# Expert products of a sparse feed-forward layer: Gelu reads them four at a time from the exponential's PSUM buffers

## The chip, the cores and the metric

The kernel runs on one core of a Trainium2 chip. The metric is the device time of the whole program in microseconds (us), lower is better. A core has the engines PE (TensorE, matmul), DVE (VectorE), ACT (ScalarE), POOL (GpSimd) and SP (SyncE, which issues the transfers here). Each runs its own instructions in order; semaphores tie them together.

## The reference

The input has 16 sequences of 512 tokens with 128 channels. An attention layer in a window comes first and is untouched by the change. The second layer, which is the subject, picks for each token and each of 8 heads the 8 best of 1024 experts by a product of keys, and sums the experts' outputs by softmax weights:

```python
sim = jnp.einsum('pbnhd,hkpd->pbnhk', q, keys)        # 2 x 8 heads x 32 keys for a token
s, i = jax.lax.top_k(sim, k)
all_scores = (sx[..., :, None] + sy[..., None, :])    # of the 8 best of either half
scores, pk = jax.lax.top_k(all_scores, k)
w_down, w_up = key_in[idx], key_out[idx]
o = jnp.einsum('bnd,bnhkd->bnhk', inputs, w_down)
o = jax.nn.gelu(o, approximate=False) * jax.nn.softmax(scores, axis=-1)
return jnp.einsum('bnhk,bnhkd->bnd', o, w_up)
```

## The kernel before

The attention stage takes some 700 us of the span; then `ffn` works through 64 tiles of 128 tokens, in 16 groups (`GROUPS`) of 4 tiles (`GT`). Nothing is gathered: all 1024 experts are computed for each token, and those not chosen get the weight zero. A tile j is tile k of group g (j = 4g + k); k = 0 and 2 are called even here, k = 1 and 3 odd.

For each tile and each of 8 heads h:

- POOL adds the 32 x 32 scores of the two halves into SUM (L795), in a ring of 16 buffers, so up to two tiles ahead. In odd tiles DVE makes the sum of the one head without a mask (L995).
- ACT takes the exponential, SUM to E (L922). E is two buffers in PSUM, used in turn, so the exponential n waits until DVE has read the one of n - 2.
- DVE compares SUM with the head's eighth best score and multiplies by E: W (L1029), called the masked product here.
- PE turns W's eight blocks of 128 x 128, summed over the heads, into WT (L1100), for all experts of the tile.

One head, `LH`, goes another way, without DVE: two passes of ACT over SUM, a shift (Prelu with a huge slope, L878, called at h = LH - 1) and the exponential (L884, at h = LH), which writes W itself. This is "the head without a mask".

At h = 1 of the next tile DVE multiplies WT by the Gelu of the expert products, GE, into CT (L1009). PE then multiplies CT by the experts' outputs (`outputs`, L1061 and L1064) into the PSUM bank MB, and ACT copies this to OUT (`finish`, L848). PE makes the next scores (`similar`, L1039) in MB too, and ACT copies them to SIM (L828). MB is a single bank: outputs, scores and expert products take turns in it, each waiting for the copy of the one ahead.

The expert products are key_in by X2T, 8 blocks (`BLK`) of 128 experts by the 512 tokens of a group, made one group ahead: two per tile (`o_block`, L1042, at h = 0 and h = 6) in MB. ACT copies each to GE (`o_copy`, L839, at h = 3 and, of the other, at h = 1 of the next tile). In the even tiles, behind the head without a mask, ACT loads the Gelu table, takes the Gelu of four copied products in one instruction of 2048 columns in place, and loads the exponential's table again (`gelus`, L834, L835). At h = 2 of tile k = 1 ACT makes BNT (L843), the next group's rows for `similar`.

The ranking of later tiles is done on DVE in ten parts (`choose`): copies of the eight best, candidates, maxima, sums, biases. The tables `EVEN_PARTS` and `ODD_PARTS` say ahead of which head's masked product each part stands. `SLOT_*` and `COPY_*` say ahead of which head PE makes a product in MB and ACT copies it. For the first group the products go to E before the loop starts, and Gelu reads them there (L856, L1052).

Of the kernel before, what the change touches and what calls it, by code (L numbers as in the profile page):

```python
# [29 lines left out]
ACT = mybir.ActivationFunctionType  # L30
# [3 lines left out]
P = 128  # L34
# [621 lines left out]
GT = 4  # L656
GN = GT * P
# [3 lines left out]
BLK = NE // P  # L661
# [1 line left out]
CAND = 20  # L663
RING = 16
WRING = 8
LH = 3
MASKED = FH - 1
SUMS_AHEAD = (0, 2)

EVEN_PARTS = ((), (), (), (), ((1, 0), (1, 1), (1, 2), (1, 3), (1, 4), (1, 5), (1, 8), (2, 0), (2, 1), (1, 9)), (), ((1, 6),), ((1, 7),))  # L670
ODD_PARTS = ((), (), ((1, 2),), ((1, 3),), ((1, 4), (1, 5)), (), ((1, 6),), ((1, 7),))

SIM0 = 2
SLOT_A, SLOT_OUT, SLOT_SIM, SLOT_B = 0, 2, 4, 6
COPY_B, COPY_A, COPY_OUT, COPY_SIM = 1, 3, 5, 7


def ffn(nc, ctx, x1, x2T, KM, key_in, key_out, gb, ident, bnst, first, out):
# [6 lines left out]
    def sem(name):  # L685
# [30 lines left out]
    E = [ps(f"E{b}", [P, NE]) for b in range(2)]  # L716
    WT = ps("WT", [P, BLK, P])
    MB = ps("MB2", [P, GN])
# [4 lines left out]

    names = ("waits_passed half_set bn_mean bn_variance bn_rstd bn_coef x1_loaded x2T_loaded bn_rows "
             "sim_product sim_copied pair_sums exp_ready weights_masked weights_turned "
             "experts_weighted out_product out_copied expert_product expert_copied gelu_ready "
             "out_stored ranked candidates top_ready top_less_max top_exp exp_sum log_sum bias_ready "
             "l_x_moved l_sums l_shifted l_weights").split()
    S = {n: sem("f_" + n) for n in names}
# [6 lines left out]
    def wait_pos(eng, s, v):  # L736

        if not isinstance(v, int) or v > 0:
            eng.wait_ge(s, v)
# [84 lines left out]
    def _(act):  # L824
# [2 lines left out]
            act.wait_ge(S["sim_product"], j + 1)  # L827
            nc.scalar.copy(SIM[q][:, :, :, :].rearrange("p a h k -> p (a h k)"), MB[:, :]).then_inc(S["sim_copied"], 1)  # L828

        def gelus(g, b, half):  # L830

            act.wait_ge(S["expert_copied"], g * BLK + (half + 1) * 4)
            o = GE[b][:, 4 * half:4 * half + 4, :].rearrange("p e n -> p (e n)")
            nc.scalar.activation(o, o, ACT.Gelu).then_inc(S["gelu_ready"], 1)  # L834
            nc.scalar.preload_act_table_set("natural_log_exp_and_others")  # L835

        def o_copy(g, b, e):
            act.wait_ge(S["expert_product"], g * BLK + e + 1)
            nc.scalar.copy(GE[b][:, e, :], MB[:, :]).then_inc(S["expert_copied"], 1)  # L839

        def bnt(g, b):
            act.wait_ge(S["x2T_loaded"], (g + 1) * 16)
# [9 lines left out]
        for e in range(BLK):  # L852
# [1 line left out]
                sim_copy(0, 0)  # L854
            act.wait_ge(S["expert_product"], e + 1)
            nc.scalar.activation(GE[0][:, e, :], E[e // 2 % 2][:, e % 2 * GN:(e % 2 + 1) * GN], ACT.Gelu).then_inc(S["expert_copied"], 1)  # L856
        act.wait_ge(S["expert_copied"], BLK)
        act.sem_inc(S["gelu_ready"], 2)
        nc.scalar.preload_act_table_set("natural_log_exp_and_others")
        sim_copy(1, 1)  # L860
        sim_copy(2, 2)
# [27 lines left out]
        def group(g, b, more):  # L889
            for k in range(GT):  # L890
                j = g * GT + k
                q = k % 2
                real = not (isinstance(g, int) and g == 0)
                nxt = more or k < GT - 1
                for h in range(FH):
                    if h == 0:
                        act.wait_ge(S["bias_ready"], j + 1)

                    if h == 2 and k == 1 and more:
                        bnt(g + 1, 1 - b)  # L900

                    if h == COPY_B and k and more:
                        o_copy(g + 1, 1 - b, 2 * k - 1)
                    if h == COPY_B and not k and real:
                        o_copy(g, b, BLK - 1)
                    if h == COPY_A and more:
                        if k == 0:
                            wait_pos(act, S["experts_weighted"], g * GT)
                        o_copy(g + 1, 1 - b, 2 * k)
                    if h == COPY_OUT and (real or k):  # L910
                        finish(j - 1, *((g, b, k - 1) if k else (g - 1, 1 - b, GT - 1)))
                    if h == COPY_SIM and (more or k < 1):
                        sim_copy(j + 3, (k + 3) % 4)
                    if h == LH - 1:
                        l_shift(j, k, q)
                    if h == LH:
                        l_exp(j, k, q)
                    else:
                        n = masked(j, h)
                        act.wait_ge(S["pair_sums"], sums_by_pool(j, h))  # L920
                        wait_pos(act, S["weights_masked"], n - 2)
                        nc.scalar.activation(E[(n - 1) % 2][:, :], SUM[(k * FH + h) % RING][:, :], ACT.Exp, bias=NB[q][:, h:h + 1]).then_inc(S["exp_ready"], 1)  # L922

                    if h == 5 and nxt:
                        small_exp(j + 1)
                    if h == 6 and nxt:
                        small_ln(j + 1)
                    if (k, h) == (2, 3) and more:
                        gelus(g + 1, 1 - b, 0)
                    if (k, h) == (0, 3) and real:  # L930
                        gelus(g, b, 1)

        steps(act, group)
        finish(GROUPS * GT - 1, GROUPS - 1, 1, GT - 1)
# [2 lines left out]
    def _(dve):  # L937
# [66 lines left out]
        def experts(j, g, b, k):  # L1004

            dve.wait_ge(S["weights_turned"], (j + 1) * FH)
            dve.wait_ge(S["gelu_ready"], (g + 1) * 2)
            wait_pos(dve, S["out_product"], j - 1)
            nc.vector.tensor_tensor(CT[k % 2][:, :, :], WT[:, :, :], GE[b][:, :, k * P:(k + 1) * P], ALU.mult).then_inc(S["experts_weighted"], 1)  # L1009

# [25 lines left out]
    def _(pe):  # L1036
# [1 line left out]

            pe.matmul(MB[:, :], BNT[b][:, k * P:(k + 1) * P], KM[:, :], start=True, stop=True).then_inc(S["sim_product"], 1)  # L1039

        def o_block(b, e):
            pe.matmul(MB[:, :], key_in[:, e * P:(e + 1) * P], X2T[b][:, :], start=True, stop=True).then_inc(S["expert_product"], 1)  # L1042


        for e in range(BLK):
# [21 lines left out]
        def group(g, b, more):  # L1067
            for k in range(GT):
                j = g * GT + k
                real = not (isinstance(j, int) and j == 0)  # L1070
                for h in range(FH):

                    if h == SLOT_A and more:
                        pe.wait_ge(S["x2T_loaded"], (g + 2) * 16)
                        pe.wait_ge(S["sim_copied"], j + 3)
                        pe.wait_ge(S["expert_copied"], (g + 1) * BLK + 2 * k)
                        o_block(1 - b, 2 * k)
                    if h == SLOT_OUT and real:
                        pe.wait_ge(S["sim_copied"], j + 3 if more or k < 2 else GROUPS * GT)
                        pe.wait_ge(S["expert_copied"], (g + 1) * BLK + (2 * k + 1 if more else 0))  # L1080
                        wait_pos(pe, S["out_copied"], j - 1)
                        outputs(j - 1, *((g, b, k - 1) if k else (g - 1, 1 - b, GT - 1)))
                    if h == SLOT_SIM and (more or k < 1):
                        pe.wait_ge(S["bn_rows"], (g + 1) if k < 1 else (g + 2))
                        pe.wait_ge(S["expert_copied"], (g + 1) * BLK + (2 * k + 1 if more else 0))
                        wait_pos(pe, S["out_copied"], j)
                        similar(j + 3, b if k < 1 else 1 - b, (k + 3) % GT)
                    if h == SLOT_B and more:
                        pe.wait_ge(S["sim_copied"], j + 4)
                        o_block(1 - b, 2 * k + 1)  # L1090
                    if h == LH:
                        pe.wait_ge(S["l_weights"], j + 1)
                    else:
                        pe.wait_ge(S["weights_masked"], masked(j, h))

                    if h == 0:
                        wait_pos(pe, S["experts_weighted"], j)

                    for e in range(BLK):
                        o = pe.matmul(WT[:, e, :], W[h % WRING][:, e * P:(e + 1) * P], ident[:, :], is_transpose=True,  # L1100
                                      start=(h == 0 and e % 4 == 0), stop=(h == FH - 1), skip_group_check=True)
                    o.then_inc(S["weights_turned"], 1)
# [62 lines left out]
```

## Time and profile before

| | us |
|---|---|
| median of 3 runs | 1681.59 (1681.23 to 1687.32) |
| profiled execution | 1680.84 |
| its span, first to last instruction | 1679.1 |

| Engine | busy us | share of span |
|---|---|---|
| DVE | 1476.9 | 88% |
| PE | 1467.7 | 87% |
| ACT | 1315.0 | 78% |
| POOL | 1269.8 | 76% |

The busy shares are averages over two stages. The rows shown further down are of the second one, which starts at about 712 us. A row of the timeline merges instructions of one kind that follow each other; a matmul in fp32 of 512 columns counts as two instructions, since it takes two passes. Records of successive instructions on one engine overlap a little, so the distance from start to start is what one instruction costs there.

### The profile page before, as it was taken

How to read it: one execution, taken by the hardware profiler on the slowest of the kernel's cores; microseconds unless marked ns; L12 is line 12 of the kernel's file. 1: busy time of each engine (PE TensorE's matmuls, PEld its weight loads, DVE VectorE, ACT ScalarE, POOL GpSimd, SP SyncE). 2: the span in 40 equal slices, each digit the busy share in tenths (PEclk: the TensorE clock that was granted, in tenths of full speed). 3: DMA queues.
4: the chain of work that ended last, by engine and by line, in shares of the span. 5: the costliest groups of instructions: out<-in, count | busy, mean ns of one | idle time of the engine just before them, and what ended most of it. 6: DMA issues, size and time to landing. Idle time of an engine off the chain costs nothing.

```text
span 1679.1 us, 33161 instructions
## 1 busy us (share of the span) xinstructions
PE 1467.7 (87%) x10688; PEld 1012.5 (60%) x10688; DVE 1476.9 (88%) x4616; ACT 1315.0 (78%) x1805; POOL 1269.8 (76%) x1547
## 2 busy tenths in 40 slices
PE   3899999999999999688888888888888888888887
PEld 2355555555555554256766767767676676767766
DVE  3899999999999986269999999999999999999997
ACT  1176666666666666479999999999999999999995
POOL 1065555555656555399999999999999999999992
PEclk9999999999999999889999999999999999999999
DMA  5344444544445541100000000000000000000000
GB/s 143 88 101 106 113 113 112 114 112 113 104 113 112 114 105 36 44 20 1 20 20 20 1 20 20 1 20 20 12 8 20 20 2 20 20 7 14 14 7 7
DMA packets 73629, 86.39 MB, mean 51 GB/s; under 512 B 9872, under 2 KB 63760, under 8 KB 68752
## 3 DMA queue, kind: packets, MB, share of 16 engines
q1 hardware_dynamic: 73456, 84.27, 21.0%
q8 instruction: 85, 1.39, 0.4%
q14 instruction: 88, 0.72, 0.2%
HBM read 58.30 MB, written 25.95 MB: 50 GB/s over the span
## 4 chain that ended last, share of the span: by engine, by line
ACT 15%; POOL 14%; DVE 12%; PE 8%; issue 8%; DVEq 0%; ACTq 0%; SPq 0%
POOL SUM L795 14%; DVE W L1029 8%; ACT E L922 7%; PE WT L1100 5%; ACT L835 2%; ACT L834 2%; PE MB L1039 1%; ACT W L884 1%; PE MB L1042 1%; DVE SMALL L975 1%; ACT SIM L828 1%; DVE M8Y L958 1%; ACT GE L834 1%; ACT GE L839 1%; DVE CD L965 0%
## 5 line engine op out<-in xcount | busy, mean ns | idle before, releaser
L795 POOL TENSOR_TENSOR SUM<-SIM 128x1024 f32<-128x1024 f32 x480 | 899.5, 1910 | 34.9 <-DVE W L1029 31.3
L1100 PEld LDWEIGHTS WT<-idf,W 128*128 128x128 f32 x4096 | 478.5, 147 | 212.3 <-issue 127.1
L1029 DVE SCALAR_TENSOR_TENSOR W<-SUM,SMALL,E 128x1024 f32<-128x1024 f32 x448 | 560.5, 1280 | 42.6 <-ACT E L922 42.2
L1100 PE MATMUL WT<-idf,W 128*128 128x128 f32 x4096 | 545.0, 284 | 57.9 <-DVE CT L1009 38.2
L261 POOL TENSOR_SCALAR_AFFINE_SELECT PT<-PT 128x128 f32<-128x128 f32 (+1 forms) x1024 | 335.2, 353 | 258.8 <-ACT PT L355 223.8
L922 ACT ACTIVATE E<-SUM,NB 128x1024 f32<-128x1024 f32 x448 | 495.4, 1116 | 20.4 <-DVE W L1029 17.0
L414 DVE CUSTOM_DVE_ANT_0 SY<-SY,bandf 128x384 f32<-128x384 f32 x512 | 273.4, 574 | 0.0
L355 ACT ACTIVATE PT<-TX 128x512 f32<-128x512 f32 x256 | 153.2, 598 | 114.5 <-PE TX L542 114.3
L429 DVE TENSOR_REDUCE mx<-SX 128x2 f32<-128x512 f32 x256 | 174.5, 682 | 56.1 <-PE SX L524 56.0
L357 ACT ACTIVATE PT<-TY 128x768 f32<-128x768 f32 x256 | 207.6, 811 | 4.1 <-PE TY L542 0.4
L570 PE MATMUL PV<-PT,V 128*32 128x384 f32 (+1 forms) x2048 | 165.8, 442 | 2.6 <-POOL PT L261 2.4
L516 PE MATMUL SY<-K,Q 72*128 72x384 bf16 x512 | 144.4, 341 | 8.6 <-DVE mx L414 4.6
L1039 PE MATMUL MB<-KM,BNT 128*128 128x512 f32 x128 | 77.0, 686 | 72.4 <-ACT OUT L848 70.6
L542 PE MATMUL TY<-Q,K 75*128 75x384 bf16 x512 | 126.9, 330 | 11.5 <-ACT PT L357 10.4
L1064 PE MATMUL MB<-KO,CT 128*128 128x128 f32 x1024 | 124.9, 276 | 1.1 <-DVE CT L1009 1.1
L516 PE MATMUL SX<-K,Q 72*128 72x256 bf16 x512 | 102.5, 283 | 21.3 <-DMA Q<-q_parts 16.0
L1064 PEld LDWEIGHTS MB<-KO,CT 128*128 128x128 f32 x1024 | 119.5, 192 | 1.3 <-DVE CT L1009 1.3
L542 PE MATMUL TX<-Q,K 75*128 75x256 bf16 x512 | 100.3, 278 | 2.3 <-ACT PT L355 2.1
L542 PEld LDWEIGHTS TX<-Q,K 75*128 75x128 bf16 x512 | 38.0, 98 | 96.2 <-issue 82.9
L570 PEld LDWEIGHTS PV<-PT,V 128*32 128x32 f32 x2048 | 53.7, 109 | 68.3 <-issue 49.9
L1009 DVE TENSOR_TENSOR CT<-WT,GE 128x1024 f32<-128x1024 f32 x64 | 78.4, 1225 | 13.5 <-PE WT L1100 13.5
L516 PEld LDWEIGHTS SX<-K,Q 72*128 72x128 bf16 x512 | 48.8, 100 | 64.2 <-issue 17.6
(116 smaller groups left out, 1854.6 us busy)
## 6 DMA issues: line engine op xcount, KB each, us to landing
K<-k_parts SPq DMA_DIRECT2D x96, 192.0 KB
Q<-q_parts SPq DMA_DIRECT2D x288, 64.0 KB
q_parts<-qp SPq DMA_DIRECT2D x16, 384.0 KB, 2.4
k_parts<-kp SPq DMA_DIRECT2D x16, 384.0 KB, 2.4
xin<-in_x SPq DMA_DIRECT2D x16, 256.0 KB, 3.2
xres<-in_x SPq DMA_DIRECT2D x16, 256.0 KB, 9.7
x<-X SPq DMA_DIRECT2D x16, 256.0 KB, 2.2
x2T<-X2T SPq DMA_DIRECT2D x16, 256.0 KB, 2.1
```

The lines of the kernel that those rows point to most:

```text
L261: return nc.gpsimd.affine_select(out=out, in_=out, compare_op=ALU.is_ge, fill=0.0, base=0, pattern=([[0, 2]] if pairs else []) + [[s, P]], ...
L357: nc.scalar.activation(pt[:, 512:1280].rearrange("p (j n) -> p j n", j=2), TY[:, :, 0:384], ACT.Exp).then_inc(S["inner_exp"], 1)
L414: return nc.vector.tensor_tensor_reduce(out=scores, in0=scores, in1=bandf[:, k0 * P:k1 * P], scale=1.0, scalar=-3e38, op0=ALU.add, op1=ALU ...
L429: nc.vector.tensor_reduce(mx[:, h, 0:4:3], SX[:, :, :], AX.X, ALU.max).then_inc(S["outer_maxima"], 1)
L516: return pe.matmul(out, Q[b][0:KQ, h, i * P:(i + 1) * P], K[b][0:KQ, h, k0 * P:k1 * P], start=clear, stop=done, skip_group_check=True)
L542: return pe.matmul(out[:, 0:(q1 - q0) * P], K[b][0:R, h, j * P:(j + 1) * P], Q[b][0:R, h, q0 * P:q1 * P], start=True, stop=True, skip_grou ...
L570: o = pe.matmul(PV[32 * e:32 * e + 32, q0 * P:q1 * P], V[b][:, slot:slot + SLOT_V], PT[:, h % 8, at:at + (q1 - q0) * P], start=(j == 0 and ...
L795: return eng.tensor_tensor(SUM[(q * FH + h) % RING][:, :].rearrange("p (i j) -> p i j", i=NK), sx, sy, ALU.add)
L922: nc.scalar.activation(E[(n - 1) % 2][:, :], SUM[(k * FH + h) % RING][:, :], ACT.Exp, bias=NB[q][:, h:h + 1]).then_inc(S["exp_ready"], 1)
L1029: nc.vector.scalar_tensor_tensor(out=W[h % WRING][:, :], in0=SUM[(k * FH + h) % RING][:, :], scalar=TOP[q][:, h, TOPK - 1:TOPK], in1=E[(n ...
L1064: o = pe.matmul(po, CT[k % 2][:, e, :], key_out[:, e, :], start=False, stop=(e == BLK - 1))
L1100: o = pe.matmul(WT[:, e, :], W[h % WRING][:, e * P:(e + 1) * P], ident[:, :], is_transpose=True, start=(h == 0 and e % 4 == 0), stop=(h == ...
```

## The change

The expert products no longer use MB or pass through a copy. In each even tile that had a Gelu (30 of the 64 tiles) PE makes four of them straight into the two E buffers: two in the buffer of head 0 once its masked product is done, two in that of head 1 once that one is done. Gelu reads them from there, 512 columns at a time, right behind the head without a mask, and writes GE. The copies (`o_copy`) are gone, 120 in all, with the waits that they put on MB. `LH` goes from 3 to 2, so that exactly two masked heads, 0 and 1, have left the buffers by then. The output product of an odd tile moves from h = 2 to h = 1, its copy stays at h = 5; in an even tile the product stays at h = 2 and its copy moves from h = 5 to h = 4. The parts of the ranking move with `LH`: in even tiles from ahead of head 4 to ahead of head 3; in odd tiles part 3 from head 3 to 4, parts 4 and 5 from head 4 to 5.

```diff
-LH = 3
+LH = 2
-EVEN_PARTS = ((), (), (), (), ((1, 0), (1, 1), (1, 2), (1, 3), (1, 4), (1, 5), (1, 8), (2, 0), (2, 1), (1, 9)), (), ((1, 6),), ((1, 7),))
-ODD_PARTS = ((), (), ((1, 2),), ((1, 3),), ((1, 4), (1, 5)), (), ((1, 6),), ((1, 7),))
+EVEN_PARTS = ((), (), (), ((1, 0), (1, 1), (1, 2), (1, 3), (1, 4), (1, 5), (1, 8), (2, 0), (2, 1), (1, 9)), (), (), ((1, 6),), ((1, 7),))
+ODD_PARTS = ((), (), ((1, 2),), (), ((1, 3),), ((1, 4), (1, 5)), ((1, 6),), ((1, 7),))
-SLOT_A, SLOT_OUT, SLOT_SIM, SLOT_B = 0, 2, 4, 6
-COPY_B, COPY_A, COPY_OUT, COPY_SIM = 1, 3, 5, 7
+SLOT_OUT, SLOT_SIM = (2, 1), 4
+COPY_OUT, COPY_SIM = (4, 5), 7
...
+    def expert_bank(j, e):
+        return E[(j * MASKED + e // 2) % 2][:, e % 2 * GN:(e % 2 + 1) * GN]
...
-        def gelus(g, b, half):
-            act.wait_ge(S["expert_copied"], g * BLK + (half + 1) * 4)
-            o = GE[b][:, 4 * half:4 * half + 4, :].rearrange("p e n -> p (e n)")
-            nc.scalar.activation(o, o, ACT.Gelu).then_inc(S["gelu_ready"], 1)
+        def gelus(j, g, b, half):
+            wait_pos(act, S["experts_weighted"], (g - 1) * GT)
+            nc.scalar.preload_act_table_set("gelu_and_others")
+            for e in range(4 * half, 4 * half + 4):
+                act.wait_ge(S["expert_product"], g * BLK + e + 1)
+                nc.scalar.activation(GE[b][:, e, :], expert_bank(j, e), ACT.Gelu).then_inc(S["expert_copied"], 1)
             nc.scalar.preload_act_table_set("natural_log_exp_and_others")
-        def o_copy(g, b, e):
-            act.wait_ge(S["expert_product"], g * BLK + e + 1)
-            nc.scalar.copy(GE[b][:, e, :], MB[:, :]).then_inc(S["expert_copied"], 1)
+            act.wait_ge(S["expert_copied"], g * BLK + 4 * half + 4)
...
                     if h == LH:
                         l_exp(j, k, q)
+                        if k == 2 and more:
+                            gelus(j, g + 1, 1 - b, 0)
+                        if k == 0 and real:
+                            gelus(j, g, b, 1)
...
+        def o_blocks(j, g, b, half, h):
+            if half == 0:
+                pe.wait_ge(S["x2T_loaded"], (g + 1) * 16)
+            pe.wait_ge(S["weights_masked"], masked(j, h))
+            for e in range(4 * half + 2 * h, 4 * half + 2 * h + 2):
+                pe.matmul(expert_bank(j, e), key_in[:, e * P:(e + 1) * P], X2T[b][:, :], start=True, stop=True).then_inc(S["expert_product"], 1)
...
+                    for hh, after in ((0, 0), (2, 1)):
+                        if h == hh and k == 2 and more:
+                            o_blocks(j, g + 1, 1 - b, 0, after)
+                        if h == hh and k == 0 and real:
+                            o_blocks(j, g, b, 1, after)
-                    if h == SLOT_OUT and real:
+                    if h == SLOT_OUT[k % 2] and real:
```

How the rows of an engine's program read: line, operation, written from read tiles with their buffer numbers, shape, how many. First ACT in an even tile of the kernel before, from the exponential of head 0 (SUM0) to the copy of OUT behind that of head 4:

```order
L922 ACTIVATE E0<-SUM0,NB0 128x1024
L839 COPY GE1<-MB2 128x512
L922 ACTIVATE E1<-SUM1,NB0 128x1024
L878 ACTIVATE SUM3<-SUM3,NT0 128x1024
L922 ACTIVATE E0<-SUM2,NB0 128x1024
L839 COPY GE1<-MB2 128x512
L884 ACTIVATE W3<-SUM3,NL0 128x1024
L834 ACT_TABLE_LOAD
L834 ACTIVATE GE1<-GE1 128x2048
L835 ACT_TABLE_LOAD
L922 ACTIVATE E1<-SUM4,NB0 128x1024
L848 COPY OUT0<-MB2 128x128
```

The same place on ACT in the changed kernel:

```order
L919 ACTIVATE E0<-SUM0,NB0 128x1024
L879 ACTIVATE SUM2<-SUM2,NT0 128x1024
L919 ACTIVATE E1<-SUM1,NB0 128x1024
L885 ACTIVATE W2<-SUM2,NL0 128x1024
L837 ACT_TABLE_LOAD
L840 ACTIVATE GE1<-E0 128x512 x2
L840 ACTIVATE GE1<-E1 128x512 x2
L841 ACT_TABLE_LOAD
L919 ACTIVATE E0<-SUM3,NB0 128x1024
L851 COPY OUT0<-MB2 128x128
L919 ACTIVATE E1<-SUM4,NB0 128x1024
```

The copies are out, and the exponential of a masked head (SUM2 before) has moved from ahead of the Gelu to behind it (SUM3 now).

Next PE in an even tile of the kernel before, from the last head of the tile ahead (W7) to the scores in MB; L1042 is an expert product:

```order
L1100 MATMUL WT<-idf,W7 128x128 x8
L1042 MATMUL MB2<-X2T1,KI 128x512
L1100 MATMUL WT<-idf,W0 128x128 x8
L1100 MATMUL WT<-idf,W1 128x128 x8
L1061 MATMUL MB2<-X1_first,idf 128x128
L1064 MATMUL MB2<-KO,CT1 128x128 x8
L1100 MATMUL WT<-idf,W2 128x128 x8
L1100 MATMUL WT<-idf,W3 128x128 x8
L1039 MATMUL MB2<-KM,BNT1 128x512
```

The same place on PE in the changed kernel; L1040 is an expert product there:

```order
L1093 MATMUL WT<-idf,W7 128x128 x8
L1040 MATMUL E0<-X2T1,KI 128x512 x2
L1093 MATMUL WT<-idf,W0 128x128 x8
L1093 MATMUL WT<-idf,W1 128x128 x8
L1040 MATMUL E1<-X2T1,KI 128x512 x2
L1059 MATMUL MB2<-X1_first,idf 128x128
L1062 MATMUL MB2<-KO,CT1 128x128 x8
L1093 MATMUL WT<-idf,W2 128x128 x8
L1093 MATMUL WT<-idf,W3 128x128 x8
L1032 MATMUL MB2<-KM,BNT1 128x512
```

Four expert products stand in this tile now, in two pairs with the transposes of heads 0 and 1 between them; the one at h = 6 and those of the odd tiles have left their places.

Last ACT in an odd tile with k = 1 of the kernel before, from the exponential of head 0 to that of head 4:

```order
L922 ACTIVATE E1<-SUM8,NB1 128x1024
L839 COPY GE0<-MB2 128x512
L922 ACTIVATE E0<-SUM9,NB1 128x1024
L843 ACTIVATE BNT0<-X2T_first,ab 128x512
L878 ACTIVATE SUM11<-SUM11,NT1 128x1024
L922 ACTIVATE E1<-SUM10,NB1 128x1024
L839 COPY GE0<-MB2 128x512
L884 ACTIVATE W3<-SUM11,NL1 128x1024
L922 ACTIVATE E0<-SUM12,NB1 128x1024
```

The same place on ACT in the changed kernel:

```order
L919 ACTIVATE E1<-SUM8,NB1 128x1024
L879 ACTIVATE SUM10<-SUM10,NT1 128x1024
L919 ACTIVATE E0<-SUM9,NB1 128x1024
L846 ACTIVATE BNT1<-X2T1,ab 128x512
L885 ACTIVATE W2<-SUM10,NL1 128x1024
L919 ACTIVATE E1<-SUM11,NB1 128x1024
L919 ACTIVATE E0<-SUM12,NB1 128x1024
```

Both passes of the head without a mask now stand ahead of the third masked exponential.

## Rows read from the trace of the kernel before

**Rows 1.** Busy time of a stretch: us, each engine's (x instructions), clock, DMA share, GB/s.

```profile
core 0: us, PE busy (x) PEld busy (x) DVE busy (x) ACT busy (x) POOL busy (x), PEclk, DMA share, GB/s
805.20:1605.02 799.82, 696.41 (x4753) 556.80 (x4752) 741.88 (x2268) 753.51 (x906) 769.10 (x411) 0.96 0.04 14
```

**Rows 2.** Instructions of line 1009 in that stretch: durations in ns, first and last start.

```profile
L1009 DVE TENSOR_TENSOR CT<-WT,GE x55: 1224/1225/1226, 805.2 to 1605.0; 128x1024 f32<-128x1024 f32 x55
```

**Rows 3.** Busy time as in rows 1: two pairs, then two odd tiles (k = 3, k = 1).

```profile
835.14:864.30 29.16, 25.05 (x177) 19.71 (x176) 27.44 (x84) 27.29 (x33) 29.16 (x17) 1.00 0.09 28
864.30:894.23 29.93, 26.22 (x177) 20.84 (x177) 27.67 (x85) 28.48 (x36) 29.93 (x17) 0.94 0.01 1
...
835.14:848.06 12.92, 12.22 (x89) 9.89 (x88) 12.33 (x34) 11.29 (x16) 12.92 (x8) 1.00 0.01 1
...
864.30:877.41 13.11, 12.36 (x89) 9.91 (x89) 12.45 (x35) 12.22 (x18) 13.11 (x8) 1.00 0.01 1
```

**Rows 4.** Waits of the same stretch: waiter, releaser, total us, times, longest.

```profile
PE MB L1039 <- ACT OUT L848: 64.0, 27, 2.4
```

**Rows 5.** Busy time around one wait of PE for OUT.

```profile
883.60:887.00 3.40, 1.11 (x11) 0.87 (x8) 3.12 (x20) 3.37 (x5) 3.40 (x3) 1.00 0.01 2
887.00:890.50 3.50, 3.41 (x10) 2.26 (x11) 3.50 (x4) 3.31 (x6) 3.50 (x3) 0.51 0.00 0
```

**Rows 6.** Timeline of DVE in an even tile: start, duration, [idle before].

```profile
848.06 1.23 DVE L1009 TENSOR_TENSOR CT<-WT,GE 128x1024 f32<-128x1024 f32 x1
849.20 2.47 DVE L1029 SCALAR_TENSOR_TENSOR W<-SUM,SMALL,E 128x1024 f32<-128x1024 f32 x2
851.59 0.84 DVE L958 MAX8 SMALL<-SIM 128x8 f32<-128x32 f32 x8
...
857.45 2.49 DVE L1029 SCALAR_TENSOR_TENSOR W<-SUM,SMALL,E 128x1024 f32<-128x1024 f32 x2 [0.54 <-ACT E L922]
...
864.31 1.23 DVE L1009 TENSOR_TENSOR CT<-WT,GE 128x1024 f32<-128x1024 f32 x1
```

**Rows 7.** Timeline of ACT in the same tile.

```profile
846.52 0.59 ACT L839 COPY GE<-MB 128x512 f32<-128x512 f32 x1
847.00 1.12 ACT L922 ACTIVATE E<-SUM,NB 128x1024 f32<-128x1024 f32 x1
848.04 1.15 ACT L878 ACTIVATE SUM<-SUM,NT 128x1024 f32<-128x1024 f32 x1
...
850.60 1.16 ACT L884 ACTIVATE W<-SUM,NL 128x1024 f32<-128x1024 f32 x1
851.77 1.28 ACT L834 ACT_TABLE_LOAD   x1
853.06 1.92 ACT L834 ACTIVATE GE<-GE 128x2048 f32<-128x2048 f32 x1
...
856.29 1.12 ACT L922 ACTIVATE E<-SUM,NB 128x1024 f32<-128x1024 f32 x1
```

**Rows 8.** Timeline of ACT and DVE in the odd tile behind it, k = 1.

```profile
864.30 0.80 ACT L843 ACTIVATE BNT<-X2T,ab 128x512 f32<-128x512 f32 x1
...
865.01 1.14 ACT L878 ACTIVATE SUM<-SUM,NT 128x1024 f32<-128x1024 f32 x1
...
866.05 1.10 ACT L922 ACTIVATE E<-SUM,NB 128x1024 f32<-128x1024 f32 x1
...
867.18 1.29 DVE L1029 SCALAR_TENSOR_TENSOR W<-SUM,SMALL,E 128x1024 f32<-128x1024 f32 x1
```

**Rows 9.** Timeline of PE in that odd tile.

```profile
869.85 1.91 PE L1100 MATMUL WT<-idf,W 128*128 128x128 f32 x16
871.59 1.02 PE L1039 MATMUL MB<-KM,BNT 128*128 128x512 f32 x2
872.45 1.80 PE L1100 MATMUL WT<-idf,W 128*128 128x128 f32 x15
```

**Rows 10.** Instructions of line 856, Gelu from PSUM ahead of the loop.

```profile
L856 ACT ACTIVATE GE<-E x8: 597/597/597, 714.9 to 722.6; 128x512 f32<-128x512 f32 x8
```

More of the change, by code:

```diff
@@ L725, in ffn @@
              "sim_product sim_copied pair_sums exp_ready weights_masked weights_turned "
-             "experts_weighted out_product out_copied expert_product expert_copied gelu_ready "
+             "experts_weighted out_product out_copied expert_product expert_copied "
              "out_stored ranked candidates top_ready top_less_max top_exp exp_sum log_sum bias_ready "
@@ L856, in _ @@
             nc.scalar.activation(GE[0][:, e, :], E[e // 2 % 2][:, e % 2 * GN:(e % 2 + 1) * GN], ACT.Gelu).then_inc(S["expert_copied"], 1)
-        act.wait_ge(S["expert_copied"], BLK)
-        act.sem_inc(S["gelu_ready"], 2)
         nc.scalar.preload_act_table_set("natural_log_exp_and_others")
@@ L900, in group @@
                         bnt(g + 1, 1 - b)
[L902 to L910, printed above, removed]
+                    if h == COPY_OUT[k % 2] and (real or k):
                         finish(j - 1, *((g, b, k - 1) if k else (g - 1, 1 - b, GT - 1)))
@@ L927, in group @@
                         small_ln(j + 1)
[L928 to L931, printed above, removed]
         steps(act, group)
@@ L1006, in experts @@
             dve.wait_ge(S["weights_turned"], (j + 1) * FH)
-            dve.wait_ge(S["gelu_ready"], (g + 1) * 2)
+            dve.wait_ge(S["expert_copied"], (g + 1) * BLK)
             wait_pos(dve, S["out_product"], j - 1)
@@ L1039, in similar @@
             pe.matmul(MB[:, :], BNT[b][:, k * P:(k + 1) * P], KM[:, :], start=True, stop=True).then_inc(S["sim_product"], 1)
-        def o_block(b, e):
-            pe.matmul(MB[:, :], key_in[:, e * P:(e + 1) * P], X2T[b][:, :], start=True, stop=True).then_inc(S["expert_product"], 1)
+        def o_blocks(j, g, b, half, h):
[4 more added lines that the diff above has]
+                pe.matmul(expert_bank(j, e), key_in[:, e * P:(e + 1) * P], X2T[b][:, :], start=True, stop=True).then_inc(S["expert_product"], 1)
         for e in range(BLK):
@@ L1071, in group @@
                 for h in range(FH):
[L1073 to L1077, printed above, removed]
-                    if h == SLOT_OUT and real:
+                    for hh, after in ((0, 0), (2, 1)):
[4 more added lines that the diff above has]
+                    if h == SLOT_OUT[k % 2] and real:
                         pe.wait_ge(S["sim_copied"], j + 3 if more or k < 2 else GROUPS * GT)
-                        pe.wait_ge(S["expert_copied"], (g + 1) * BLK + (2 * k + 1 if more else 0))
                         wait_pos(pe, S["out_copied"], j - 1)
@@ L1084, in group @@
                         pe.wait_ge(S["bn_rows"], (g + 1) if k < 1 else (g + 2))
-                        pe.wait_ge(S["expert_copied"], (g + 1) * BLK + (2 * k + 1 if more else 0))
                         wait_pos(pe, S["out_copied"], j)
                         similar(j + 3, b if k < 1 else 1 - b, (k + 3) % GT)
-                    if h == SLOT_B and more:
-                        pe.wait_ge(S["sim_copied"], j + 4)
-                        o_block(1 - b, 2 * k + 1)
                     if h == LH:
```

## The prediction, made before the changed kernel ran

> **What bounds the kernel now.** I read three views in this order: the busy time of each engine over the feed-forward stage, the waits, and the timeline of one pair of tiles on each engine. The first [rows 1] shows no engine that is full: over 799.82 us POOL is busy 769.10, ACT 753.51, DVE 741.88, PE 696.41. So the bound is a loop of engines that wait for each other, and only a timeline tells which wait ends last. The stage repeats in pairs of tiles, an even one with a Gelu and an odd one without. The product CT (L1009) runs once per tile; its 55 starts from 805.2 to 1605.0 bound 27 pairs, 29.62 us each [rows 1, 2]. The starts of CT cut every tile below: zero is the start of CT in that tile.
>
> Two kinds of pair stand side by side [rows 3]: 29.16 us with a granted clock of 1.00, and 29.93 with 0.94. By the starts of CT one pair in three is of the first kind, 9 of the 27. In all of them PE waits up to 2.4 us for ACT's copy of OUT, 27 times, 64.0 us [rows 4]. In the second kind PE's clock stands at 0.51 instead of 1.00 for a few us right behind that wait [rows 5]: of its two levels, 1.2 GHz instead of 2.4.
>
> An even tile, in its undisturbed form, takes 16.25 us (848.06 to 864.31) [rows 6]. ACT is the late one there. It does the second masked exponential, the shift, another exponential, a copy, the exponential of the head without a mask, a table load, the Gelu of 2048 columns, a table load [rows 7]; DVE fills that stretch with its ranking of the next tiles and still idles 0.54 us before its next masked product, at 9.39 [rows 6]. An odd tile takes 13.11 where BNT is made and 12.92 elsewhere [rows 3]; DVE is busy 12.33 of 12.92, ACT 11.29 [rows 3]. So in odd tiles DVE is the bound and ACT has room; in even tiles ACT's Gelu block is the bound. POOL is up to two tiles ahead and only waits.
>
> **Part 1: the copies of expert products go.** Four ACT copies a pair leave. Each occupies a slot of 0.48 us (846.52 to 847.00) [rows 7], 1.9 us a pair. The two in the odd tile lie where ACT has room: worth nothing. The two in the even tile are ahead of the Gelu: up to 0.96. The two-pass products themselves only move, so PE's sum is unchanged; a product takes 0.86 of PE (871.59 to 872.45) and its result is there after 1.02 [rows 9].
>
> **Part 2: the Gelu block of the even tile.** One Gelu of 1.92 becomes four that read PSUM, 0.60 each [rows 7, 10]. No row has two of these back to back; bounds are 3 x 0.48 + 0.60 = 2.04 (spaced like the copies) and 4 x 0.60 = 2.39. (The Trainium skill, page "ScalarE: Activation LUTs", section "What ACT_TABLE_LOAD costs", gives an activation with immediate operands about 186 ns plus 0.833 ns a column and an overlap of 93 ns, which makes an estimate of 2.17 for four; the trace's 597 ns for one stands near its 613.) But ACT alone doesn't set this block: the third and fourth products come late.
>
> ACT's side. The shift takes the slot of the copy at 846.52, that is -1.54. Slots of shift and exponential are 1.04 (847.00 to 848.04), the one ahead of the load 1.17, the load 1.29 [rows 7]. So exponential 1 starts at -0.50, the unmasked head at 0.54, the load at 1.71, the first Gelu at 3.00.
>
> PE's side. The first two products wait for masked product 0, which ends as CT starts: 0.25 and 1.11. Transposes of heads 0 and 1 follow at 1.97 and 2.84 (0.87 a head, from 1.74 for two, 869.85 to 871.59 [rows 9]); CT, over at 1.23, doesn't hold them. Products three and four start at 3.71 and 4.57, and the last is there at 5.59. Its Gelu ends at 6.23, the load at 7.53, and exponential 3 starts then. DVE's product follows an exponential's start by 1.16 (856.29 to 857.45) [rows 6, 7]: 8.69, against 9.39 before. That is 0.70 earlier. But with the unmasked head moved from 3 to 2, only heads 0 and 1 are masked by then, not 0, 1 and 2: one masked product, 1.24 (849.20 to 851.59, two with their step), has moved behind the block. DVE, which used to have 0.54 idle, now is done with its ranking at 7.61 and idles 1.1. Masked product 5 then needs an exponential that can't start before product 3 frees its buffer, about 0.1 more. Even tile: -0.70 + 1.24 + 0.09 = +0.63, 16.88 us.
>
> **Part 3: the odd tile.** The same work on DVE, with one part of the ranking moved; a pair of short operations less lies back to back, 0.1 gained. The tile with k = 3: 12.8. With k = 1 BNT stands on ACT ahead of the unmasked head. It takes 0.71 (864.30 to 865.01), after which came shift and exponential, and DVE's second product began at 2.87 (867.18) instead of 2.72: it was just in time [rows 8]. Ahead of the exponential that DVE needs stood a copy (0.48), an exponential, BNT and the shift; now it is the shift, an exponential, BNT and the unmasked head, so the copy's slot has become one of 1.04. Exponential 1 starts at -0.49, BNT at 0.56, the unmasked head at 1.27, exponential 3 at 2.31, and DVE's product at 3.47: 0.75 behind its place. No slack behind it takes that up, since DVE is the bound. So 13.5 against 13.1 before: +0.45.
>
> Sum without the clock: 30 even tiles x 0.63 = 18.9; 15 tiles with BNT x 0.45 = 6.8; 15 without, x -0.12 = -1.8; together +23.9 against an undisturbed kernel. (First and last tiles have no Gelu and stay.)
>
> **Part 4: PE's clock.** The wait of 2.37 on OUT disappears, since outputs in the even tile end at about 7.5, behind the late products, and their copy runs as soon as the Gelus are over. PE then idles 1.7 (8.3 to 10.0) for masked product 3, and later 0.9 and 1.45 around the last transposes and CT, with one head's transposes between. If the drops stay away, the 0.42 that they cost on average (29.62 less the 29.2 of the undisturbed form) come back: 30 x 0.42 = -12.6, and the sum is +11.3. Bounds on new drops: none at all, or one in each pair, at the 0.65 or so that a drop costs now [rows 3]. The idle of 2.35 in two pieces around CT is of the size of today's 2.37, but split; I take one pair in three: 30 / 3 x 0.65 = +6.5. The sum is +17.8 us on the profiled execution's 1680.84, 1698.6; the median shown is 0.75 above that execution, so 1699.
>
> **The rivals.** (a) No drops at all: +11.3, 1693. For it: no single idle stretch of PE is as long as 2.37 any more. The Trainium skill ("TensorE: Matmul & The Clock Gate", "Why this matters for your kernels") asks to keep PE's pauses between bursts short and puts the fall of the clock down to long ones; by that rule this kernel would run undisturbed. The trace agrees in that the clock falls behind the longest wait. (b) Drops in every pair, behind CT in the odd tile, where they delay the similarity product that ACT must copy: +11.3 + 19.5 = +30.8, 1712. (c) The other side, faster: PE's late products don't hold the Gelus. If they are there by 4.5 the fourth Gelu ends at 5.07, the exponential starts at 6.36, the masked product at 7.52: even tile 16.25 - 1.87 + 1.33 = 15.71, or -0.54. Then 30 x -0.54 + 5 - 12.6 is -24, with some drops -17: about 1662. It decides at 4.48 for the result of product four, and PE's rows put that at 5.59; in between it is proportional, and break-even needs 5.2 without drops. Against it: the order of PE's instructions has two transposes of heads between the pairs of products. (d) The change moves work that isn't on the path and the shifts of DVE and ACT cancel: 1682. For it: ACT's room in the odd tiles; against it: the head that moves behind the block.
>
> **How the numbers follow.** Forecast 1699, one to two drops in five pairs: 0.45. Rival (a) 0.23, near the edge of what can be told from no change. (b) 0.10. (c) 0.08. (d) 0.14. A difference of 0.5%, 8.4 us, is about what a measurement of this kernel can tell. Slower: 0.45 + 0.10 + most of (a) = 0.72; within 0.5%: (d) and some of (a), 0.20; faster: 0.08. The range leaves out (c) and the ends of (b) and (d): 1684 to 1712.
>
> **What would show it.** In an even tile the third Gelu should wait for PE (some 0.6 and 0.4 us of ACT idle, releaser the product on E), the exponential behind the second load should start 7.5 after CT, DVE should idle 1.1 before masked product 3, and the tile should last 16.9. The odd tile with BNT should last 13.5 and show DVE waiting for ACT before its second product, about 0.75. PE's wait for OUT should be gone. It is wrong if the even tile is at or under 16.25, or if the drops of the clock come at another rate; the former breaks part 2, the latter part 4.

## The result, and the profile after

The changed kernel is slower: 1705.55 us median of 4 runs (1702.29 to 1711.65) against 1684.45 of 4 before, a ratio of 1.0132 with an interval of [1.0109, 1.0155]. Forecast were 1699 and +1.0%. The profiled execution took 1702.29, its span is 1700.6. Ratios here and below are of fast runs alone: one run of x_bnt_late (3613.85 us) and one of x_head3 (4969.86) are left out of them, and without these two the medians shown below would be 1694.12 and 1689.58.

From the first CT to the 61st, 30 pairs, before took 887.4 us and after 907.5: +20.1 in the loop. The first CT itself came 2.4 later in this execution (748.68 for 746.28). It lies between 746.3 and 753.1 in the traces of all the kernels here, whatever their loop, so I don't count that as the change. (Behind the 61st CT the execution was 1.1 shorter; the three add up to the 21.45 between the two profiled executions.)

The instructions of the line of CT, from its page of instructions, answer to [rows 2]; 27 pairs in 817.4 us are 30.27 each. Under them two pairs, one odd tile with k = 1, and the waits of that stretch, as in [rows 3, 4].

```profile
L1002 DVE TENSOR_TENSOR CT<-WT,GE x55: 1224/1224/1227, 809.2 to 1626.6; 128x1024 f32<-128x1024 f32 x55
```

```profile
839.82:870.35 30.53, 26.12 (x176) 21.72 (x176) 27.55 (x85) 25.92 (x33) 30.53 (x17) 0.94 0.09 27
900.70:930.30 29.60, 24.70 (x176) 20.06 (x176) 27.47 (x85) 25.88 (x33) 28.12 (x16) 1.00 0.09 27
930.32:943.81 13.49, 10.70 (x84) 9.26 (x84) 12.34 (x35) 11.29 (x15) 13.49 (x8) 1.00 0.01 2
```

```profile
PE WT L1093 <- DVE W L1022: 89.5, 131, 1.6
...
DVE W L1022 <- ACT E L919: 61.4, 101, 1.0
...
PE WT L1093 <- DVE CT L1002: 38.0, 27, 1.4
...
ACT OUT L851 <- PE MB L1062: 31.4, 20, 2.4
ACT E L866 <- DVE D L971: 27.6, 21, 2.0
ACT GE L840 <- PE E L1040: 24.6, 54, 0.7
```

ACT has lost work (28.48 or 27.29 us a pair before, 25.9 now) and it waits for everybody: for products, for OUT's product, for the ranking. PE's wait for OUT [rows 4] is gone; its longest pauses are now 1.6, for masked product 3, and 1.4, for CT.

An even tile on ACT (timeline: start, duration, idle before; CT is at 913.51), which answers to [rows 7]:

```profile
913.01 1.10 ACT L919 ACTIVATE E<-SUM,NB 128x1024 f32<-128x1024 f32 x1
914.05 1.14 ACT L885 ACTIVATE W<-SUM,NL 128x1024 f32<-128x1024 f32 x1
915.21 1.28 ACT L837 ACT_TABLE_LOAD   x1
916.50 1.09 ACT L840 ACTIVATE GE<-E 128x512 f32<-128x512 f32 x2
918.20 0.60 ACT L840 ACTIVATE GE<-E 128x512 f32<-128x512 f32 x1 [0.62 <-PE E L1040]
919.06 0.60 ACT L840 ACTIVATE GE<-E 128x512 f32<-128x512 f32 x1 [0.26 <-PE E L1040]
919.68 1.28 ACT L841 ACT_TABLE_LOAD   x1
920.97 1.12 ACT L919 ACTIVATE E<-SUM,NB 128x1024 f32<-128x1024 f32 x1
```

The same tile on DVE and on PE, as [rows 6] and in place of the PE rows of the prediction:

```profile
913.51 1.23 DVE L1002 TENSOR_TENSOR CT<-WT,GE 128x1024 f32<-128x1024 f32 x1
...
922.13 3.82 DVE L1022 SCALAR_TENSOR_TENSOR W<-SUM,SMALL,E 128x1024 f32<-128x1024 f32 x3 [0.96 <-ACT E L919]
...
930.32 1.23 DVE L1002 TENSOR_TENSOR CT<-WT,GE 128x1024 f32<-128x1024 f32 x1
```

```profile
913.58 1.98 PE L1040 MATMUL E<-X2T,KI 128*128 128x512 f32 x4
915.40 1.91 PE L1093 MATMUL WT<-idf,W 128*128 128x128 f32 x16
917.14 1.88 PE L1040 MATMUL E<-X2T,KI 128*128 128x512 f32 x4
...
923.47 1.09 PE L1093 MATMUL WT<-idf,W 128*128 128x128 f32 x8 [1.56 <-DVE W L1022]
```

And DVE in the odd tile behind it (CT at 930.32), which answers to [rows 8]:

```profile
933.74 1.29 DVE L1022 SCALAR_TENSOR_TENSOR W<-SUM,SMALL,E 128x1024 f32<-128x1024 f32 x1 [0.62 <-ACT E L919]
```

The Gelus wait twice for products that stand behind the transposes of two heads; DVE idles 0.96 ahead of masked product 3, which is the first of three in a row now, where it was the first of two. In the odd tile DVE waits 0.62 ahead of its second product, behind BNT and the head without a mask on ACT.

### The profile page after: what moved, and what is told of

It is laid out like the page before. It is cut to its first block, busy times and chain, and to the rows that moved or that the text cites. A ratio compares the mean times of both kernels' runs of the same rounds, so it can differ in the third digit from the quotient of the medians.

```text
span 1700.6 us, 33023 instructions
## 1 busy us (share of the span) xinstructions
PE 1456.6 (86%) x10688; PEld 1021.2 (60%) x10688; DVE 1479.2 (87%) x4616; ACT 1266.3 (74%) x1775; POOL 1271.4 (75%) x1547
## 4 chain that ended last, share of the span: by engine, by line
PE 14%; POOL 12%; issue 11%; ACT 11%; DVE 10%; DVEq 0%; ACTq 0%; SPq 0%
POOL SUM L799 12%; ACT E L919 8%; DVE W L1022 7%; PE E L1040 7%; PE WT L1093 5%; PE MB L1062 1%; ACT SIM L832 1%; DVE CT L1002 1%; ACT W L885 1%; DVE Z L975 1%; DVE SMALL L968 1%; ACT BNT L846 0%; ACT L841 0%; DVE M8Y L951 0%; PE E L1050 0%
## 5 line engine op out<-in xcount | busy, mean ns | idle before, releaser
L1093 PE MATMUL WT<-idf,W 128*128 128x128 f32 x4096 | 526.6, 279 | 155.6 <-DVE W L1022 108.9
L1093 PEld LDWEIGHTS WT<-idf,W 128*128 128x128 f32 x4096 | 462.8, 143 | 248.9 <-DVE W L1022 156.1
L1062 PE MATMUL MB<-KO,CT 128*128 128x128 f32 x1024 | 136.7, 291 | 1.1 <-DVE CT L1002 1.1
L1062 PEld LDWEIGHTS MB<-KO,CT 128*128 128x128 f32 x1024 | 132.8, 210 | 1.3 <-DVE CT L1002 1.3
L840 ACT ACTIVATE GE<-E 128x512 f32<-128x512 f32 x120 | 68.4, 596 | 27.6 <-PE E L1040 27.3
L516 PEld LDWEIGHTS SY<-K,Q 72*128 72x128 bf16 x512 | 50.5, 99 | 50.8 <-DVE mx L414 44.5
```

The costliest lines, as they stand in the source:

```text
L516: return pe.matmul(out, Q[b][0:KQ, h, i * P:(i + 1) * P], K[b][0:KQ, h, k0 * P:k1 * P], start=clear, stop=done, skip_group_check=True)
L1062: o = pe.matmul(po, CT[k % 2][:, e, :], key_out[:, e, :], start=False, stop=(e == BLK - 1))
```

## Experiments

Tile times below are distances from CT to CT in the traces. "Undisturbed" is the value that repeats where the clock is 1.00; drops are stretches of half the full clock between the first and the last CT; "30 pairs" is the time from the first CT to the 61st. Both are of one execution of each kernel. The kernel before was measured again beside each group of kernels, hence its range; a ratio is within a group, so the ratios compare better than the medians.

| kernel | median us | ratio to before | even | odd k=1 | odd k=3 | drops | 30 pairs |
|---|---|---|---|---|---|---|---|
| before | 1681.98 to 1684.45 | 1 | 16.25 | 12.90 to 13.08 | 12.90 | 20 | 887.4 |
| changed | 1705.55 | 1.0132 [1.0109, 1.0155] | 16.84 | 13.49 | 12.79 | 15 | 907.5 |
| x_products_first | 1690.29 | 1.0050 [1.0033, 1.0068] | 16.45 | 13.49 | 12.79 | 15 | 896.0 |
| x_bnt_late | 1695.98 | 1.0076 [1.0057, 1.0096] | 16.83 | 12.79 | 12.79 | 8 | 896.7 |
| x_clock_filler | 1693.26 | 1.0075 [1.0050, 1.0099] | 16.84 | 13.49 | 12.79 | 0 | 899.8 |
| x_both | 1664.76 | 0.9900 [0.9876, 0.9924] | 15.78 | 12.79 | 12.79 | 14 | 869.5 |
| x_both_filler | 1652.12 | 0.9821 [0.9794, 0.9847] | 15.78 | 12.79 | 12.79 | 0 | 858.3 |
| x_both_filler_scores | 1653.34 | 0.9816 [0.9790, 0.9843] | 15.72 | 12.80 | 12.80 | 1 | 856.1 |
| x_before_short_odd | 1686.81 | 1.0019 [1.0006, 1.0033] | 16.25 | 12.91 | 12.91 | 20 | 888.6 |
| x_before_short_even | 1669.27 | 0.9921 [0.9899, 0.9943] | 15.79 | 12.91 | 12.91 | 16 | 872.4 |
| x_head3 | 1689.75 | 1.0047 [1.0032, 1.0062] | 16.17 | 12.91 | 12.90 | 22 | 895.5 |
| x_head3_filler | 1667.07 | 0.9905 [0.9888, 0.9922] | 16.17 | 12.91 | 12.90 | 1 | 873.0 |

In the kernel before the 20 drops lie in even tiles, some 9.4 to 11.3 us behind CT, where PE has waited for OUT; in the changed one the 15 lie in odd tiles, 1.2 to 1.8 behind CT. The last of these 15 comes after the 61st CT, so 14 count for the 30 pairs.

**Products first.** Both pairs of products ahead of the transposes:

```diff
-                    for hh, after in ((0, 0), (2, 1)):
-                        if h == hh and k == 2 and more:
+                    for after in (0, 1):
+                        if h == 0 and k == 2 and more:
...
-                        if h == hh and k == 0 and real:
+                        if h == 0 and k == 0 and real:
```

> The changed kernel with one edit: PE makes the third and fourth expert products right behind the first two, ahead of the transposes of heads 0 and 1. Theory (the Gelus wait for PE's late products): the last product is there at 4.4 us after CT instead of 5.35, the exponential behind the second table load starts at 6.4 instead of 7.46, DVE's masked product 3 comes when its ranking is over, at 7.66 instead of 8.62. But the output product ends at 8.2 now, and its copy stands ahead of exponential 4 on ACT, so masked product 4 comes at 9.6 instead of 9.9: even tile 16.5 instead of 16.84, some 9 us less than the changed kernel (1696). Rival (the Gelu block with its table loads is itself too long, whoever feeds it): the exponential stays near 7.4 and the time within 2 us of the changed kernel.

ACT's four Gelus now run without a wait (CT at 909.46):

```profile
912.45 2.10 ACT L840 ACTIVATE GE<-E 128x512 f32<-128x512 f32 x4
...
915.86 1.12 ACT L919 ACTIVATE E<-SUM,NB 128x1024 f32<-128x1024 f32 x1
917.71 0.27 ACT L851 COPY OUT<-MB 128x128 f32<-128x128 f32 x1 [0.73 <-PE MB L1062]
```

The exponential starts at 6.40 after CT. The even tile fell by 0.39, and the next thing in line is the one expected: the copy of OUT waits 0.73 with the exponential behind it. The loop lost 11.5 us, 11.7 of it by the even tiles (30 x 0.39). The theory holds; its rival is out.

**BNT late.**

```diff
-                    if h == 2 and k == 1 and more:
+                    if h == 5 and k == 1 and more:
                         bnt(g + 1, 1 - b)
```

> The changed kernel with one edit: in the odd tile with k = 1 ACT makes BNT ahead of the copy of OUT at h = 5 instead of ahead of the head without a mask. Theory: BNT alone makes that tile 13.49 instead of 12.79, since it stands ahead of the exponential that DVE needs and there are two passes of ACT now where one was; moved into ACT's idle time it costs nothing, 15 x 0.7 = 10.5 us less than the changed kernel (1695). Rival (ACT's order in the odd tile does not matter, the tile with k = 1 is long for another reason such as PE's wait for BNT or the clock): within 2 us of the changed kernel.

The odd tiles are 12.79, apart from those with a drop and three of 12.93 to 13.09. In its new place BNT fills a wait of ACT (932.56 to 933.38, straight into OUT's copy). The loop lost 10.9, 15 tiles x 0.7 = 10.5. Only 8 drops are left, but each costs 0.92 now, so the clock costs about what it did (7.4).

**A filler for the clock.** Behind the transposes of the last head, in even tiles:

```diff
+                    if h == FH - 1 and k % 2 == 0 and more:
+                        pe.wait_ge(S["sim_copied"], j + 4)
+                        pe.matmul(MB[:, :], BNT[b][:, k * P:(k + 1) * P], KM[:, :], start=True, stop=True)
```

> The changed kernel with one instruction more in each even tile: PE makes a product of 512 columns into the free bank MB behind the last transposes, in the pause before CT; nobody reads it. Theory (PE's pauses around CT bring its clock down in about 17 of 29 pairs, which costs 0.22 us in an odd tile with BNT and 0.92 in one without): no clock of 1.2 GHz in the loop, all odd tiles 12.79 or 13.49, some 9 us less than the changed kernel (1696). Rival (the clock has no part in it, the long odd tiles come from the queue of PE): 26 products more, the same or a longer time.

PE idles twice around CT in the changed kernel, with one head's transposes between; this is the stretch ahead of a drop (CT at 839.84):

```profile
838.70 1.09 PE L1093 MATMUL WT<-idf,W 128*128 128x128 f32 x8 [0.77 <-DVE W L1022]
841.21 1.58 PE L1093 MATMUL WT<-idf,W 128*128 128x128 f32 x8 [1.41 <-DVE CT L1002]
```

The odd tile behind this CT (k = 3) took 13.71. Its PE, ACT and DVE, and the clock early in it:

```profile
843.01 2.91 PE L1062 MATMUL MB<-KO,CT 128*128 128x128 f32 x16
...
848.38 1.02 PE L1032 MATMUL MB<-KM,BNT 128*128 128x512 f32 x2
```

```profile
849.44 0.59 ACT L832 COPY SIM<-MB 128x512 f32<-128x512 f32 x1 [0.50 <-PE MB L1032]
```

```profile
851.08 2.48 DVE L1022 SCALAR_TENSOR_TENSOR W<-SUM,SMALL,E 128x1024 f32<-128x1024 f32 x2 [1.00 <-ACT E L919]
```

```profile
840.50:844.00 3.50, 2.79 (x15) 2.82 (x16) 3.50 (x10) 3.06 (x3) 3.50 (x3) 0.66 0.00 0
```

The output product takes 2.91 instead of 1.95, the scores come late, ACT waits 0.50 for them and DVE 1.00 instead of the usual 0.34 to 0.39. With the filler the pause of 1.41 is one of 0.55, the one of 0.77 stays, and the clock is 1.00 over 800 us:

```profile
927.04 1.02 PE L1098 MATMUL MB<-KM,BNT 128*128 128x512 f32 x2
928.61 1.07 PE L1093 MATMUL WT<-idf,W 128*128 128x128 f32 x8 [0.55 <-DVE CT L1002]
```

```profile
805.00:1605.00 800.00, 684.32 (x4747) 541.48 (x4746) 734.52 (x2239) 700.80 (x866) 759.26 (x407) 1.00 0.04 14
```

The 14 drops within the 30 pairs were worth 7.7 us, 0.55 each. An odd tile with BNT loses 0.22, since DVE is late there anyway, one without 0.92; seven drops fell on each kind. The 17 of 29 pairs in the expectation were a misreading: the trace has 14 of 30. The pairs without a drop have the same two pauses; what picks the pairs stays open here.

**Together.** The two edits, and `COPY_OUT` from (4, 5) to (5, 5):

> The changed kernel with three edits: products three and four behind the first two, the copy of OUT in the even tile at h = 5 behind exponential 4 instead of ahead of it, and BNT late. Theory: masked product 3 at 7.66, nothing late behind it, even tile 16.84 - 0.96 = 15.9; odd tile 12.8; some 29 + 10 = 39 us less than the changed kernel, 1667, and so about 18 less than the kernel before. Rival (another wait takes the place, PE's output product and the scores behind it): even tile over 16.3 and the time at or over the kernel before.

```profile
913.06 3.81 DVE L1022 SCALAR_TENSOR_TENSOR W<-SUM,SMALL,E 128x1024 f32<-128x1024 f32 x3
```

DVE goes from its ranking into masked product 3 without a pause. 38.0 us less in the loop than the changed kernel, for 39 expected, and 1% faster than the one before. All 14 drops fell on odd tiles with k = 1 (13.6 to 13.7 for 12.79). They cost 0.86 each there, where the same tile lost 0.22 as long as BNT made DVE late anyway. PE's longest pauses in this kernel are 1.4, for CT, and 0.8, for a masked product:

```profile
PE WT L1093 <- DVE W L1022: 43.6, 95, 0.8
PE WT L1093 <- DVE CT L1002: 39.4, 28, 1.4
```

So:

> Products first, OUT's copy at h = 5, BNT late, and the idle product of 512 columns on PE behind the last transposes of even tiles. Theory: the kernel without the filler has its 14 drops of the clock nearly all in tiles with k = 1, each costing 0.86 us (13.65 instead of 12.79); with the filler none, so 12 us less than without it, 1653. Rival (those tiles are 13.65 for a reason in the order of ACT or DVE): no change against the one without the filler.

No drops, 12.6 us less in the median: the fastest version by its median, 1.8% under the kernel before. Two things limit what this says. The kernel before was never run with a filler. By its undisturbed tiles (30 x 16.25 + 15 x 13.08 + 15 x 12.90) its loop would be 877.2 without drops, an estimate; so some 19 of the 29.1 us come from the order of the work and 10 from the clock. And POOL, which only waited in the kernel before, has next to no room left:

```profile
805.00:1600.00 795.00, 712.70 (x4950) 563.05 (x4950) 761.50 (x2346) 725.20 (x904) 790.89 (x423) 1.00 0.05 14
```

It is busy 790.89 of 795 us, 1.87 a sum; its 15 sums a pair are 28.05 of the 28.61 that a pair takes. A better order alone can give little more than this 0.56 a pair.

A last edit, the copy of the scores behind exponential 7:

> The same, with ACT's copy of the scores behind exponential 7 instead of ahead of it. DVE idles 0.34 to 0.39 us ahead of masked product 7 in every tile, since exponential 7 waits for the logarithm and this copy. Theory: exponential 7 comes 0.47 earlier, but the next tile's exponential 0 stays where it was and becomes the late one by 0.2, so 0.15 us less in each of 64 tiles, about 9 us less than without this edit, 1644. Rival (the slot only moves, no gain): the same time as without it.

This is a miss: 2.2 us in the loop instead of 9, and nothing in the median. DVE's wait ahead of product 7 is gone, but the copy shifts ACT's exponentials 0 to 3 of the next tile by 0.23, and DVE pays ahead of the next products:

```profile
919.78 1.28 DVE L1022 SCALAR_TENSOR_TENSOR W<-SUM,SMALL,E 128x1024 f32<-128x1024 f32 x1 [0.24 <-ACT E L917]
...
923.93 1.28 DVE L1022 SCALAR_TENSOR_TENSOR W<-SUM,SMALL,E 128x1024 f32<-128x1024 f32 x1 [0.16 <-ACT E L917]
```

I had followed the slot to the next exponential and no further.

**What the copies cost.** In the kernel before, `n` instead of 512 columns in `o_copy` (`k % 2 == 0` in the second of the two runs):

```diff
+            n = 8 if k % 2 == 1 else GN
-            nc.scalar.copy(GE[b][:, e, :], MB[:, :]).then_inc(S["expert_copied"], 1)
+            nc.scalar.copy(GE[b][:, e, 0:n], MB[:, 0:n]).then_inc(S["expert_copied"], 1)
```

> The kernel before, with the copies of expert products in odd tiles cut to 8 of their 512 columns (what is left out of GE is zero or old, so the outputs are not the reference's; a memset of one GE buffer ahead of the loop is added). It asks what the copies of the odd tiles cost. Theory (ACT has room in the odd tile, DVE is the bound): odd tiles stay at 12.9, those of 13.08 with BNT become 12.9, even tiles stay; 0 to 2 us less than the kernel before, not measurable. Rival (each ACT copy is on the loop): 0.4 us for each of 60 copies, 24 us less.

> The same cut in the even tiles only (again outputs that are not the reference's). It asks what removing copies is worth if no head is moved and PE's products come early. Theory: 0.76 us of ACT go from ahead of the Gelu block, DVE's ranking has 0.54 of slack, so the even tile falls from 16.25 to 15.7 in its undisturbed form; 30 x 0.54 = 16 us less, and up to 12 more if the shorter wait of PE for the copy of OUT keeps the clock up: 1654 to 1666. Rival (the bound of the even tile is elsewhere, PE or POOL): within 4 us of the kernel before.

In odd tiles they cost nothing: no gain, rather 2.6 us more in the median. Some 2 us of that are the memset that this kernel has ahead of the loop, 3.51 us on POOL: POOL's first sum starts 6.2 us behind the instruction that writes `rb`, 4.1 before. A few odd tiles stayed at 13.05 to 13.09, against my expectation; as I read it, the exponential ahead of BNT waits there for DVE to free its buffer and not for the copy. In even tiles they cost 0.46 of each tile, 15.1 us in the loop; DVE's wait of 0.54 ahead of its masked product is gone. The time, 1669.27, is above the 1654 to 1666 expected (it has the same memset). The clock gained little from it: PE's wait for OUT went from 2.4 to 2.2 at most and the drops from 20 to 16:

```profile
PE MB L1042 <- ACT OUT L850: 51.9, 27, 2.2
```

**The head's place.** `x_both` with `LH = 3`, the ranking's tables of before, and the products in the buffers of heads 1 and 2, made ahead of the transposes of head 1:

```diff
-LH = 2
+LH = 3
...
-        return E[(j * MASKED + e // 2) % 2][:, e % 2 * GN:(e % 2 + 1) * GN]
+        return E[(j * MASKED + 1 + e // 2) % 2][:, e % 2 * GN:(e % 2 + 1) * GN]
...
-            pe.wait_ge(S["weights_masked"], masked(j, h))
+            pe.wait_ge(S["weights_masked"], masked(j, h + 1))
...
-                        if h == hh and k == 2 and more:
+                        if h == 1 and k == 2 and more:
```

> The three edits of the kernel with products first (both pairs of products together, OUT's copy at h = 5, BNT late), but the head without a mask stays at 3 with the ranking where it was before, and the products use the buffers of heads 1 and 2. It asks what moving that head from 3 to 2 is worth by itself. Theory (masked product 2 ends only at 3.7 after CT, so the second pair of products is there at 6.2 and the exponential behind the block starts at 8.1, masked product 4 at 9.3): even tile 16.1 where LH = 2 has 15.8, odd tile 12.8 to 12.9; some 8 to 12 us more than the kernel with LH = 2, 1673 to 1677, still below the kernel before. So the move of the head is not what makes the changed kernel slow. Rival (moving a masked product behind the block is a loss of its own): the even tile is shorter than 15.8 and the time under 1665.

The undisturbed tiles are as expected, the time isn't: twelve even tiles of 17.3 to 17.5 (the ten in the next expectation are a miscount) and ten odd ones of 13.6 to 13.7. In one of the even tiles (CT at 819.1) the clock is 0.62 around the products, and all four Gelus wait, 0.23, 0.57, 0.26 and 0.26; the second:

```profile
820.00:823.40 3.40, 2.96 (x10) 2.09 (x11) 3.40 (x12) 3.38 (x4) 3.40 (x3) 0.62 0.00 0
```

```profile
824.95 0.60 ACT L840 ACTIVATE GE<-E 128x512 f32<-128x512 f32 x1 [0.57 <-PE E L1040]
```

> The kernel with the head without a mask at 3, plus the idle product of 512 columns on PE behind the last transposes, in even and odd tiles (its tile has no expert product ahead of CT in either). The run without it came out at 1689.75 instead of the 1673 to 1677 expected; its undisturbed even tiles were 16.14 to 16.21 as expected, but ten were 17.3 to 17.5. Theory (drops of PE's clock did that, at 1.3 us where they meet the four expert products): no drops, even tiles 16.1 to 16.2, odd 12.9, 1664 to 1667, some 12 more than the kernel with LH = 2 and filler (1652). Rival (the long even tiles come from the order of the work): they stay, 1689.

With the filler, now in all tiles, 22.7 us less, 1667.07 where 1664 to 1667 was expected. So `LH = 2`, with the ranking's places that go with it, is better by 0.39 an even tile and 0.12 an odd one once the products are early, 14.6 us of the loop. What was bad about the change was what it put ahead of the late products and ahead of the exponential that DVE needs. Where the head would be better with the late products wasn't run.

## Why the prediction was right

The direction and the range held, and so did the mechanism: the undisturbed tiles came out within 0.07 us, with the waits where they had been forecast. Part 4 held in its mechanism but not in its rate, and some of the closeness of the sum is luck, since errors cancel.

- **Part 1**, the copies: nothing in odd tiles, up to 0.96 of ACT in even ones. Held: 0 and, capped by DVE's slack, 0.46.
- **Part 2**, the even tile: 16.88 forecast, 16.81 to 16.87 measured. The last Gelu ended at 6.15 after CT (6.23), exponential 3 started at 7.46 (7.53), product 3 at 8.62 (8.69), DVE idled 0.96 (1.1), ACT 0.62 and 0.26 for products (0.6 and 0.4). Making the products first removed ACT's waits for them and brought the exponential to 6.40.
- **Part 3**, the odd tile: 13.5 and 12.8 forecast, 13.49 and 12.79 measured; DVE waits 0.62 ahead of its second product there (0.75). Moving BNT gave the difference back. The 13.11 taken for the tile of before with BNT holds behind an undisturbed even tile alone; behind one with a drop it is 12.90.
- **Part 4**, the clock. PE's wait for OUT is gone as forecast, and its drops with it, but they had cost less than I took: 887.4 against 877.2 for the undisturbed tiles, 10.2 and not 12.6, since the mean undisturbed pair is 29.24 and not 29.2, and the mean of all 30 pairs 29.58 and not the 29.62 of the 27. New drops: ten at 0.65 forecast, 14 in the 30 pairs at 0.55 measured, 7.7 for 6.5. By the prediction's own sign (drops at another rate) this breaks part 4 in its rate: one pair in two and not one in three. The price had been taken from a pair of before, where the low clock met another part of the tile; it depends on what is late anyway in the tile that it meets: 0.22 with BNT, 0.92 without, 1.3 on the products of x_head3.

In sum the loop changed by +22.6 in undisturbed tiles (x_clock_filler's 899.8 less 877.2; forecast +23.9), -10.2 by the old drops (-12.6) and +7.7 by the new ones (+6.5): +20.1 against +17.8. The median is 6.6 above the 1699 forecast; 2.9 of that is the kernel before, whose median stood at 1681.59 for the forecast and at 1684.45 beside the changed kernel.

Of the rivals, (a), no drops, is refuted by the 15 drops; with the filler that condition was made, and the time came out at its 1693 (1693.26). The Trainium skill, in "TensorE: Matmul & The Clock Gate", "Why this matters for your kernels", warns of pauses longer than any of these. The measurements decide against taking that as a bound: one pause of 2.4 in the kernel before, and two of 0.77 and 1.41 with a single head's transposes between them in the changed one, each had the clock fall behind them in about half of the pairs or more (20 and 14 of 30). Rival (c), the products early, was the mechanism from which a gain had to come. As an experiment alone it took 0.39 off the even tile, and 1.06 together with OUT's copy at h = 5 (x_both). Rival (b), a drop in every pair, is out too. So is (d), no change: the interval of the ratio lies above 1.

## What to carry to other kernels

An engine that is relieved gives time back only as far as the next engine's slack; here 0.46 us of 0.96, and only in one tile of two. A producer's place in its own queue can decide more than the copy that is saved: list what stands ahead of it there. Where two engines alternate in a tight loop, follow a moved slot around the whole loop, to the same instruction one tile later, before its gain is counted. And look at the engine that only waits, here POOL: it sets how far the others can be sped up.

## What I had not expected of the hardware

In these traces PE's clock falls behind split pauses (0.77 and 1.41, 14 drops in x_both, which has no longer one) as well as behind one long one (2.4 in the kernel before). A single product of 512 columns that nobody reads, placed in the pause, keeps the granted clock at 1.00 (15 drops to 0, 14 to 0, 22 to 1; in the third case it stands in every tile). It was worth 7.7, 11.2 and 22.5 us of the loop. A stretch of low clock cost from 0.2 to 1.3 us by what it met.
